# State-space conv taps of B and C as multiply-adds on VectorE, squares paired on GpSimd, and another PSUM bank for a transposition in linear attention

## What is computed

```
zxbcdt = x @ W_in.T                       # z: 256, x: 256, B: 128, C: 128, dt: 4 heads
dt  = softplus(zxbcdt[..., 768:] + dt_bias)
xBC = conv(xBC, conv_w, width 4, causal, one filter per channel)
xBC = silu(xBC + conv_b)                  # split into xs (256), B (128), C (128)
state = state * exp(dt * A) + dt * B * x  # scan over the 128 rows
y = (state . C) + D * xs
y = rmsnorm(y * silu(z), norm_w) @ W_out.T
```

## Time and profile before

| what | us |
|---|---|
| median of 3 runs | 4474.85 (4472.83 to 4477.2) |
| the profiled execution's own time | 4476.7 |
| its span | 4475.0 |
| linear attention, first to last transposition of x | 22.9 to 498.4 |
| state space, weights' preparation | 2716 to 2762 |
| state space, 64 batches | 2762 to 3686 |
| PE, DVE, ACT, POOL busy over the span | 4064.2, 2950.7, 2773.7, 1789.5 |

### The profile page before, as it was taken

The page is one execution under the profiler, slowest core; times in us unless marked ns, Lnnn a source line. Parts: engine busy times, 40 slices in busy tenths (PEclk is TensorE's granted clock), DMA queues, the critical chain, the costliest instruction groups (busy, mean ns, idle before and its releaser), DMA issues. The chain is left out here.

```text
span 4475.0 us, 110467 instructions
## 1 busy us (share of the span) xinstructions
PE 4064.2 (91%) x35464; PEld 3177.9 (71%) x35464; DVE 2950.7 (66%) x7412; ACT 2773.7 (62%) x6382; POOL 1789.5 (40%) x1808
## 2 busy tenths in 40 slices
PE   6888799999799997879999786999999998998999
PEld 4666588888566665756666565888888886775777
DVE  5777655555399997459999554555555547775665
ACT  5666455555499997349999532555555556775333
POOL 3322122222289997028888301333333331111444
PEclk9999899999899999999999998999999999999999
DMA  0000000000000000000000000000000000000000
GB/s 15 9 8 9 19 7 6 6 6 6 17 15 16 15 16 19 27 25 17 16 16 16 23 24 17 1 0 0 0 0 0 0 2 5 3 3 18 12 12 12
DMA packets 138633, 49.26 MB, mean 11 GB/s; under 512 B 105066, under 2 KB 137644, under 8 KB 138540
## 3 DMA queue, kind: packets, MB, share of 16 engines
q1 hardware_dynamic: 138540, 48.06, 4.3%
HBM read 18.72 MB, written 4.19 MB: 5 GB/s over the span
## 5 line engine op out<-in xcount | busy, mean ns | idle before, releaser
L1155 POOL TENSOR_TENSOR l_rc<-l_rc,l_rs 128x1024 f32<-128x1024 f32 x128 | 303.4, 2371 | 118.8 <-DVE l_rs L1356 115.5
L1229 ACT ACTIVATE l_prob<-l_prob,l_mx 128x128 f32<-128x128 f32 x1024 | 311.8, 388 | 0.0
L1725 POOL TENSOR_TENSOR mb_r<-mb_r,mb_projb 128x128 f32<-128x128 f32 x64 | 84.8, 1325 | 503.0 <-DVE mb_xn L1981 503.0
L783 POOL TENSOR_TENSOR ca_prob<-ca_prob,ca_sm 128x1232 f32<-128x1232 f32 x64 | 143.9, 2249 | 299.7 <-DVE ca_sm L949 299.7
L1254 PE MATMUL l_qk_ps<-l_wqkv,l_hT 128*128 128x512 f32 x512 | 248.6, 609 | 12.9 <-DVE l_rs L1356 11.4
L1841 PE MATMUL mb_bc_ps<-mb_xT,mb_wbc 128*128 128x128 f32 x2048 | 256.6, 280 | 1.8 <-ACT mb_xT L1748 1.8
L1140 POOL TENSOR_TENSOR l_prob<-l_prob,l_sm 128x1024 f32<-128x1024 f32 x128 | 242.8, 1897 | 16.4 <-DVE l_sm L1342 15.6
L1123 POOL TENSOR_TENSOR l_rc<-l_rc,l_ss 128x1024 f32<-128x1024 f32 x128 | 243.4, 1902 | 12.6 <-POOL l_rc L1155 4.6
L1841 PEld LDWEIGHTS mb_bc_ps<-mb_xT,mb_wbc 128*128 128x128 f32 x2048 | 241.8, 194 | 2.3 <-ACT mb_xT L1748 2.3
L1868 PE MATMUL mb_x_ps<-mb_wx,mb_xT 128*128 128x256 f32 x1024 | 231.6, 379 | 0.0
L1447 ACT ACTIVATE m_gl<-m_ps,m_b 128x256 f32<-128x256 f32 (+1 forms) x192 | 76.2, 468 | 227.6 <-PE m_ps L1466 227.6
(11 more groups left out here) (367 smaller groups left out, 12055.2 us busy)
## 6 DMA issues: line engine op xcount, KB each, us to landing
l_h<-lt_y SPq DMA_DIRECT2D x256, 32.0 KB
m_hin<-lt_hn SPq DMA_DIRECT2D x64, 128.0 KB, 2.0
l_h<-lt_y SPq DMA_DIRECT2D x256, 31.8 KB
la_xin<-in_x SPq DMA_DIRECT2D x64, 64.0 KB
out_x<-k_x SPq DMA_DIRECT2D x64, 64.0 KB, 1.5
ca_ctxT<-in_ctx_T SPq DMA_DIRECT2D x128, 19.2 KB, 2.0
l_wqkv<-in_L_ffn_wqkv SPq DMA_DIRECT2D x2, 768.0 KB
ca_ctx<-in_ctx SPq DMA_DIRECT2D x64, 19.2 KB
```

The lines of the kernel that those rows point to most:

```text
L783: gp.tensor_tensor(prob[b.slot][:], prob[b.slot][:], sm[b.lane][:, 1].unsqueeze(2).to_broadcast([T, H, S]), ALU.mult).then_inc(*pool_prob. ...
L1155: gp.tensor_tensor(wide(rc[l][:]), wide(rc[l][:]), wide(rs[l][:]), ALU.add).then_inc(*pool_sum.did("rot"))
L1229: ex = sc.activation(p[:, a, j], p[:, a, j], ACT.Exp, bias=mx[l][:, a, j:j + 1])
```

## The change

In the state-space stage:

- B and C of both directions (`SHIFTED`, all four blocks) get one product each with the unshifted xT (L1862 of the new kernel), 4 in place of 16. ScalarE multiplies each result by the last tap and adds the bias (`pre`, 4 instructions of 128x128, Identity). VectorE adds the other three taps of each block as multiply-adds from PSUM over 127, 126 and 125 columns (`conv`, L1941): 12 instructions. One silu of 128x512 then replaces four of 128x128.
- The 12 stand in `softplus`: 8 between the steps of the chain, 4 behind dta. m (now `decayed`) also stands in it, behind z2. The series has 5 terms with fitted coefficients in place of 7.
- On VectorE xb moves ahead of r, xn, acc and x.
- ScalarE squares u as before; GpSimd adds the squares in pairs (`uq`, 128x256), and the products with ones are 2 in place of 4 and follow the output product. On GpSimd `uq` comes first in a step and `steps` ahead of the bias and residual.
- The products of y are written in pairs of heads: two with `decay`, then two with `ddiag`.
- Preparation: 16 scalings of weights in place of 32, 20 transpositions in place of 32.

In linear attention the normalised x is turned into the unused last 128 columns of `front` and waits for qkv of VectorE in place of `attT`.

```diff
@@ linear attention, TensorE
                     if b:
                         te.wait_ge(*pool_norm.at("xn", b))
-                        if at(OUT):
-                            te.wait_ge(*act_att.at("attT", at(OUT)))
...
-                        te.transpose(turned[:, 3], xn[b.lane][:], g.ident[:]).then_inc(*pe_norm.did("xnT"))
+                        te.wait_ge(*act_turn.at("xnT", b, ago=1))
+                        if at(QKV):
+                            te.wait_ge(*vec_qkv.at("qkv", at(QKV)))
+                        te.transpose(front[:, 3 * C:4 * C], xn[b.lane][:], g.ident[:]).then_inc(*pe_norm.did("xnT"))
@@ state space, GpSimd
+                    b = at(OUT)
+                    if b:
+                        pairs = usq[b.lane][:].rearrange("p (k a) t -> p k a t", a=PAIRS)
+                        gp.wait_ge(*act_out.at("usq", b))
+                        gp.wait_ge(*pe_out.at("out", b, ago=2))
+                        gp.tensor_tensor(uq[b.lane][:], pairs[:, :, 0], pairs[:, :, 1], ALU.add
+                                         ).then_inc(*pool_out.did("uq"))
@@ state space, ScalarE
+                        sc.wait_ge(*pe_proj.at("bc", b))
+                        sc.wait_ge(*act_proj.at(SILU, b, ago=2))
+                        for i, (k, a) in enumerate(SHIFTED):
+                            sc.activation(pre[b.lane][:, i], bc_ps[:, T * i:T * i + T], ACT.Identity,
+                                          bias=cbbc[:, k, a:a + 1], scale=cw[:, k, 2 + a, TAPS - 1:TAPS]
+                                          ).then_inc(*act_conv.did(f"t0{i}"))
...
-                        for i in range(4):
-                            k, a = i // 2, i % 2
-                            sc.activation(bc[l][:, k, a], bc_ps[:, T * i:T * i + T], ACT.Silu, bias=cbbc[:, k, a:a + 1]
-                                          ).then_inc(*act_proj.did(f"sb{i}"))
+                        sc.wait_ge(*vec_conv.at(f"t{TAPS - 1}{NSH - 1}", b))
+                        sc.activation(two(bc[l][:].rearrange("p k a t -> p (k a) t")), two(pre[l][:]), ACT.Silu
+                                      ).then_inc(*act_proj.did("sb"))
@@ state space, TensorE
-                            for j in range(TAPS):
-                                at_j = starts[k][j]
-                                mm = te.matmul(bc_ps[:, T * i:T * i + T], wbc[:, k, j, a], xT[l][:, at_j:at_j + T],
-                                               start=(j == 0), stop=(j == TAPS - 1))
+                        for i, (k, a) in enumerate(SHIFTED):
+                            mm = te.matmul(bc_ps[:, T * i:T * i + T], wbc[:, k, 0, a], here, start=True, stop=True)
                         mm.then_inc(*pe_proj.did("bc"))
@@ state space, VectorE
+                def conv(b, back, i):
+                    k = SHIFTED[i][0]
+                    here, there = slice(back, T), slice(0, T - back)
+                    if k == 1:
+                        here, there = there, here
+                    out = pre[b.lane][:, i, here]
+                    if back == 1:
+                        v.wait_ge(*act_conv.at(f"t0{NSH - 1}", b))
+                    else:
+                        v.wait_ge(*vec_conv.at(f"t{back - 1}{i}", b))
+                    v.scalar_tensor_tensor(out=out, in0=bc_ps[:, T * i + there.start:T * i + there.stop],
+                                           scalar=cw[:, k, 2 + SHIFTED[i][1], TAPS - 1 - back:TAPS - back], in1=out,
+                                           op0=ALU.mult, op1=ALU.add).then_inc(*vec_conv.did(f"t{back}{i}"))
```

More of the change, by code:

```diff
@@ L1528, in mamba @@
     PAD = TAPS - 1
-    TERMS = 7
+    SHIFTED = ((0, 0), (0, 1), (1, 0), (1, 1))
+    NSH = len(SHIFTED)
+    TERMS = 5
+    series_of = lambda w: sum(w ** (n - 1) / (2 * n + 1) for n in range(1, 30))
+    fit = np.polynomial.chebyshev.Chebyshev.interpolate(series_of, TERMS - 1, domain=[0.0, 1.0 / 9.0])
+    series_fit = fit.convert(kind=np.polynomial.Polynomial, domain=[-1, 1], window=[-1, 1]).coef
     d = g.d
@@ L1681, in mamba @@
         vec_x = Stage(m.sem("vec_x"), "xb")
+        vec_conv = Stage(m.sem("vec_conv"), " ".join(f"t{back}{i}" for back in range(1, TAPS) for i in range(NSH)))
+        act_conv = Stage(m.sem("act_conv"), " ".join(f"t0{i}" for i in range(NSH)))
         vec_seg = Stage(m.sem("vec_seg"), "gm m")
@@ L1696, in mamba @@
         pool_seg = Stage(m.sem("pool_seg"), "xdt")
+        pool_out = Stage(m.sem("pool_out"), "uq")
         NORM, TURN, PROJ, SEG, OUT = range(5)
+        ORDER = [*SHIFTED, *[c for c in ((0, 0), (0, 1), (1, 0), (1, 1)) if c not in SHIFTED]]
+        SILU = "sb"
         one = lambda b: flat(g.x[:, bass.ds(b.index, 1), :])
@@ L1721, in step @@
                                          ).then_inc(*pool_seg.did("xdt"))
+                    b = at(PROJ)
+                    if b:
+                        gp.wait_ge(*vec_dt.at("dta", b))
+                        gp.wait_ge(*pe_seg.at("seg", b, ago=2))
+                        gp.tensor_tensor(by_dir(steps[b.lane][:]), per_head(upto[:]), per_step(dta[b.lane][:]), ALU.mult
+                                         ).then_inc(*pool_dt.did("steps"))
                     b = at(NORM)
@@ L1727, in step @@
                         gp.tensor_tensor(one(b), one(b), r[b.lane][:], ALU.add).then_inc(*pool_norm.did("xr"))
[L1728 to L1733, removed]
                 pipeline(gp, g.NB, OUT + 2, step)
@@ L1738, in _ @@
             def _(sc):
-                for stage in (act_norm, act_turn, act_dt, act_proj, act_seg, act_out):
+                for stage in (act_norm, act_turn, act_conv, act_dt, act_proj, act_seg, act_out):
                     stage.start(sc)
@@ L1932, in softplus @@
                     v.tensor_tensor(dta[b.lane][:], dt[b.lane][:], nega[:], ALU.mult).then_inc(*vec_dt.did("dta"))
+                    for back, i in taps:
+                        conv(b, back, i)
                 def step(at):
@@ L1970, in step @@
                     if b:
-                        softplus(b)
+                        softplus(b, at(SEG))
+                    elif at(SEG):
+                        decayed(at(SEG))
+                    b = at(PROJ)
+                    if b:
+                        l = b.lane
+                        v.wait_ge(*pe_proj.at("x", b))
+                        v.wait_ge(*pe_seg.at("y", b, ago=2))
+                        v.tensor_tensor(two(xs[l][:]), x_ps[:], two(cbx[:]), ALU.add).then_inc(*vec_x.did("xb"))
                     b = at(NORM)
@@ L1998, in step @@
                                                op0=ALU.mult, op1=ALU.add).then_inc(*vec_out.did("x"))
-                    b = at(PROJ)
-                    if b:
-                        l = b.lane
-                        v.wait_ge(*pe_proj.at("x", b))
-                        v.wait_ge(*pe_seg.at("y", b, ago=2))
-                        v.tensor_tensor(two(xs[l][:]), x_ps[:], two(cbx[:]), ALU.add).then_inc(*vec_x.did("xb"))
                 pipeline(v, g.NB, OUT + 2, step)
```

107 lines of the change are left out of this document (61 added, 46 removed).

## The result

The changed kernel takes 4332.7 us (median of 4 runs, 4331.4 to 4334.0), the kernel before 4475.2 us beside it: a ratio of 0.968, with a 95% interval of 0.967 to 0.970. The profiled execution took 4332.66 us with a span of 4331.0. The forecast was 4350, with a range of 4258 to 4424.

What follows compares the result with a forecast made beforehand. TensorE was taken to set the state-space step (14.30 us), and a ring through x afterwards (12.78). 4476.7 - 94 (state space) - 24 (linear attention) - 7 (preparation) = 4351.7, forecast as 4350 us, range 4258 to 4424.

Steps and rivals of the forecast that it cites:

- a ring through x: State-space loop: x, transposition, seg, g, bc, dt, VectorE's chain and taps, xb, r, xn, acc, x; 12.78 us a step.
- The ring's length: State-space step: sum of pieces from x's end round to the next, 12.40 us, or 12.78 with r's wait.
- den to r: VectorE's chain, m, twelve taps at 0.26 us, nine small steps and xb: 6.66 us of the state-space step.
- The wait for `steps`: State-space step: VectorE's r is kept out until GpSimd's `steps` ends, 0.38 us, with 0 as the other end.
- Starts 12.8 us apart: Sign on TensorE's row in the state-space stage: successive transpositions start 12.8 us apart.
- The sum: State-space saving: 14.30 - 12.78 = 1.52 us a step over 62 steady steps, 94 us.
- Linear attention: Without the wait for attT, m0 to m1 takes 2.50 us, 0.40 less a step over some 60 steps: 24 us.
- Preparation: Weight preparation: fewer scalings and transpositions save 7 us, between 3 and 10.
- TensorE stays the bound: Rival, state-space stage: the step goes towards TensorE's own 11.1 us, giving 4277 to 4246 us; chance 0.27.
- The taps cost their full length: Rival, VectorE in the state-space stage: 0.35 us a tap, step at most 14.1 us, middle 4393 us; chance 0.17.
- the slower rival: State-space stage: GpSimd lies across VectorE's chain (1.0 us), taps and chain do not overlap; step 15.6 us, 4524 us; chance 0.05.

Runs made afterwards that it cites:

- e1: The changed kernel with acc and x placed ahead of r and xn on VectorE: 4292.8 us.
- e8: e1's kernel without the four taps at distance three, so part of the convolution is left out: 4243.8 us.
- e3: The changed kernel with r placed ahead of xb on VectorE, so that it meets GpSimd's `steps` earlier: 4398.6 us.
- e7: The changed kernel without the four taps at distance three, so xb and r follow dta directly: 4322.4 us.
- e4: The changed kernel with linear attention as it was before the change: 4358.7 us.
- e2: The changed kernel with acc and x placed behind dta, ahead of the last three taps, a tap between them: 4320.2 us.
- e5: e1's kernel with GpSimd computing xdt ahead of uq: 4265.6 us.

## Why the prediction was right

The time came out 17 us under the forecast. The mechanism is the one forecast; several terms were off, in both directions, and in part they made up for each other.

- **TensorE is freed, a ring through x takes over.** As forecast, by the transposition's row (idle until VectorE's k_x, 1.05 and 1.19 us), and shown by e1, which shortens the step by moving acc and x alone, and e8, in which the idle time is gone. The forecast was 1 to 2 us.
- **The ring's length.** Piece by piece, in us, for the two steps from 3050.59 to 3075.78, whose main rows are shown above:

  | piece | forecast | step with the branch | step without |
  |---|---|---|---|
  | end of x to the transposition | 0.07 | 0.14 | 0.05 |
  | transposition to v | 3.54 | 4.11 | 3.56 |
  | v to den | 0.65 | 0.64 | 0.64 |
  | den to r | 6.66 | 6.28 | 6.24 |
  | r's wait for `steps` | 0.38 | 0.18 | 0.18 |
  | r to the end of x, without that wait | 1.48 | 1.54 | 1.63 |
  | sum | 12.78 | 12.89 | 12.30 |

  The largest term that was mis-sized is den to r. A tap costs 0.26 as worked out, but a step of the chain ahead of a tap 0.07 and not 0.12. The nine small steps take 0.65 us where 1.05 was worked out, 0.40 less. The 0.12 was read from dta to r. e8 shows it from dta to xb in one of two steps (3046.59 to 3046.71), and 0.07 in the other (3057.69 to 3057.76); from a step to a tap it is 0.07 throughout.
- **The wait for `steps`.** Its mechanism stood on GpSimd's rows only and was taken to hold the other way. e3 and e7 show that it does: r ends 0.08 us behind `steps` at 0.53, 1.12 and 1.48 us of length. Its size was 0.18 and not 0.38. `steps` ended 2.14 us behind dta's start, as worked out, and r was due at 1.69 (worked out: 1.76). But the sum let r begin when `steps` ends, with its whole 0.35 us behind that. In fact it ends 0.08 behind `steps`, so 0.27 of it pass within the wait.
- **"Starts 12.8 us apart".** 12.39 and 12.78 by turns, mean 12.58. The branch was not in the sum. From the transposition to v the step behind it takes 4.11 us and the other 3.56, so it adds some 0.3 to the mean. That the mean came within 0.2 of the forecast is in part luck: this missing term and the too long chain have opposite signs.
- **The sum.** (14.30 - 12.58) x 62 is 107 us and not 94; the fill gave 3 more.
- **Linear attention.** Forecast 24, found 27.4 by the checkpoints and 26 by e4. L520 follows L513 without a gap, m0 to m1 is 2.57 (forecast 2.50). Luck again: in the steady steps of the kernel before this distance goes between 2.90 and 3.09 us, 3.01 in the mean, and the forecast counted from the shortest. So the gain a step is 0.44 and not 0.40, which over some 60 steps is the 27 us measured.
- **Preparation.** 6.5 of 7 us.
- **The rivals.** "TensorE stays the bound" did not happen, but its floor is there: 11.18 us (e8). "The taps cost their full length" fell with the 0.33 us period of tap and step. GpSimd across the chain, the slower rival's mechanism, does not happen in the changed kernel's steady steps (av 0.17; q lasts 0.60 us in every second one, but v starts 0.33 behind dt in both, so it costs nothing). It did in e1 and cost some 0.35 us a step there, a third of what that rival had it at, and in e2 av alone lasted 0.68 us longer.

The Trainium skill (SBUF — State Buffer, SBUF: two separate sides) says of the engine that comes second that "the other fully blocks". The runs agree for VectorE as the second, 1.12 us for an instruction of 0.34 in e3 and 1.48 in e7, and the taps, which read PSUM, keep their 0.35 us beside `steps`. r has one tensor in SBUF as its input, so of the conditions that the prediction quotes it would be the 2-port mode; no run here shows the mode.

## What to carry to other kernels

When work moves off the engine that is full, write down the ring that closes through the last instruction of the engine that takes it, and put on that ring first what the full engine waits for: here x ahead of r and xn gave 40 us. Leaving out four taps gave 10 in the old order, since a wait stood behind them, and 49 in the new one. So order the ring first, and then count what its work costs. Look, too, where GpSimd's long instructions fall beside VectorE's short ones on the ring: two instructions of GpSimd in another order gave 27 us.

## What the runs showed of the hardware

- **A wait inside a record.** VectorE's instruction that GpSimd keeps out is not shown as waiting. It starts on time and lasts longer: q 0.99 us in place of 0.21 on 128x1 (e1), av 0.85 in place of 0.17 on 128x8 (e2), r up to 1.54 in place of 0.34 on 128x128 (e7). A line whose median and least differ is the place to look; the waits listed for these lines do not name GpSimd.
- **The clock at short pauses.** With pauses of 1.69 and 0.30 us in every second step (e3), TensorE's granted clock fell in 24 of these steps, and each fall cost 1.65 us. In five others, with the same 1.69 and 0.34 us, it stayed at 1.00, so the pauses do not settle it alone. With 1.19 and 0.32 us (the changed kernel) it did not fall in the steady part. The steps of e3 are 1.06 us longer in the mean, 0.40 of it the longer ring and the rest the clock.
- **The branch.** Idle time of 0.3 us shows on TensorE in every second step when it comes to the branch late (the changed kernel, e1, e5), and none when it is full (e8: 11.15 to 11.21 us in every step).
